# One attention kernel: maxima sent by SyncE, three score banks, one values bank, and new step offsets

## The reference, cut to what matters

```python
qh = q.reshape(b * h, d // h, m); kh = ...; vh = ...        # d = 128 channels, h = 8 heads of 16
qk = jnp.einsum('bdm,bdn->bmn', qh, kh) * scale             # 256 x 256 scores a head
sm = jax.nn.softmax(qk, axis=-1)
ret = jnp.einsum('bmn,bcn->bcm', sm, vh)
x = x + ret
```

## Time and profile before

| | us |
|---|---|
| median of 3 runs (451.76 to 454.36) | 451.77 |
| the profiled execution's own time | 453.62 |
| its span in the trace | 451.8 |
| start, up to the first transposed scores | 0 to 43.7 |
| the 128 steps and the end of the first block | 43.7 to 284 |
| choice of the tokens by digits | 284 to 326 |
| second attention and feed-forward | 326 to 451.8 |

### The profile page before, as it was taken

One profiled execution on the slowest core, in us unless ns is written; L12 is line 12 of the kernel. 1 busy time (PEld: TensorE's weight loads), 2 busy tenths in 40 slices (PEclk: granted clock), 3 DMA queues, 4 the chain that ended last, 5 costly groups with the idle time before them and its releaser, 6 DMA issues.

```text
span 451.8 us, 6847 instructions
## 1 busy us (share of the span) xinstructions
PE 293.6 (65%) x1888; PEld 185.2 (41%) x1888; DVE 298.2 (66%) x925; ACT 170.7 (38%) x413; POOL 113.1 (25%) x248
## 2 busy tenths in 40 slices
PE   0053764777667878767986764100157999999996
PEld 0011422343333443434442422000135888888884
DVE  6855565457666875768775453888747788878641
ACT  3201632334554465534354651000011455565622
POOL 1101662233322434222122221000013333332300
PEclk9999966668888695899685995555555799999999
DMA  3876584662925719245000047000000000000001
GB/s 97 194 186 113 137 166 83 155 107 93 159 49 146 135 51 180 54 114 111 0 2 1 3 127 245 1 1 0 0 0 1 1 23 2 23 23 23 23 25 46
DMA packets 24106, 32.80 MB, mean 73 GB/s; under 512 B 3915, under 2 KB 22158, under 8 KB 22542
## 3 DMA queue, kind: packets, MB, share of 16 engines
q1 hardware_dynamic: 23566, 32.34, 31.4%
q10 hardware_dynamic: 512, 0.13, 0.2%
HBM read 23.88 MB, written 8.39 MB: 71 GB/s over the span
## 4 chain that ended last, share of the span: by engine, by line
DVE 33%; PE 33%; issue 11%; DMA 8%; ACT 5%; ACTq 4%; POOL 4%; SPq 2%; DVEq 1%; POOLq 0%
PE pv_bank L1054 7%; DVE row_max L574 6%; DVE denom_inv L592 5%; PE scoret_bank L1040 4%; ACTq L886 4%; DMA q_stack<-q_parts_dram 4%; PE t_bank L1237 4%; PE score_bank L1027 4%; PE pv_bank L1155 3%; ACT probs L875 2%; DMA q_parts_dram<-q_parts 2%; PE score_bank L1218 2%; POOL rstd L390 2%; DVE junk L685 1%; DVE denom_own L596 1%
## 5 line engine op out<-in xcount | busy, mean ns | idle before, releaser
L574 DVE TENSOR_REDUCE row_max<-score_bank 128x2 f32<-128x512 f32 x112 | 73.5, 675 | 65.0 <-PE score_bank L1027 64.6
L875 ACT ACTIVATE probs<-scoret_bank 128x512 f32<-128x512 f32 x128 | 74.2, 600 | 77.0 <-issue 50.8
L1040 PE MATMUL scoret_bank<-q_stack,k_stack 98*128 98x256 bf16 x256 | 61.1, 332 | 53.4 <-ACT probs L875 44.5
L1027 PE MATMUL score_bank<-k_stack,q_stack 96*128 96x256 bf16 x240 | 57.7, 337 | 23.3 <-DMA q_stack<-q_parts_dram 16.1
L1040 PEld LDWEIGHTS scoret_bank<-q_stack,k_stack 98*128 98x128 bf16 x256 | 24.8, 114 | 75.7 <-ACT probs L875 57.6
L1054 PE MATMUL pv_bank<-probs,values_ones 128*32 128x256 f32 x512 | 48.6, 514 | 0.0
L1027 PEld LDWEIGHTS score_bank<-k_stack,q_stack 96*128 96x128 bf16 x240 | 21.4, 114 | 56.5 <-DVE row_max L574 21.5
L388 POOL TENSOR_SCALAR var_eps<-mv 128x1 f32<-128x1 f32 x48 | 9.1, 190 | 137.1 <-DVE mv L743 78.3
L1155 PE MATMUL pv_bank<-q_stack,k_stack 128*128 (+1 forms) x256 | 35.8, 283 | 0.4 <-ACT q_stack L1003 0.4
L978 ACT COPY xnt<-score_bank 128x256 f32<-128x256 f32 x16 | 6.0, 373 | 75.4 <-PE score_bank L1176 75.4
L1155 PEld LDWEIGHTS pv_bank<-q_stack,k_stack 128*128 128x128 f32 x256 | 33.7, 201 | 1.3 <-issue 0.9
(11 more groups left out here) (191 smaller groups left out, 542.2 us busy)
## 6 DMA issues: line engine op xcount, KB each, us to landing
q_stack<-q_parts_dram SPq DMA_DIRECT2D x48, 128.0 KB, 7.0
k_parts_dram<-k_parts SPq DMA_DIRECT2D x24, 128.0 KB
q_parts_dram<-q_parts SPq DMA_DIRECT2D x24, 128.0 KB
k_stack<-k_parts_dram SPq DMA_DIRECT2D x8, 384.0 KB, 4.9
ctx_stage<-in_ctx_dram SPq DMA_DIRECT2D x8, 256.0 KB, 3.3
x_stage<-in_x_dram SPq DMA_DIRECT2D x8, 256.0 KB, 4.2
k_stack<-k_parts_dram SPq DMA_DIRECT2D x8, 256.0 KB, 5.5
xs<-in_x_dram SPq DMA_DIRECT2D x8, 256.0 KB, 7.8
```

Source lines behind the costliest of these rows:

```text
L574: dve.tensor_reduce(row_max[:, i, :, h], score_bank[bank_of][:, :].rearrange("p (m n) -> p m n", m=2), AX.X, ALU.max).then_inc(s["max_done ...
L875: act.activation(probs[:, j % PROBS, :], scoret_bank[j % 2][:, :], ACT.Exp).then_inc(s["exp_done"], 1)
L1027: ins = pe.matmul(to[:, m * D:(m + 1) * D], q_stack[0:QROWS, slot, h, b_in, m * P:(m + 1) * P], k_stack[0:QROWS, slot, h, b_in, :], start= ...
L1040: ins = pe.matmul(scoret_bank[j % 2][:, k * D:(k + 1) * D], k_stack[0:SROWS, slot, h, b_in, k * P:(k + 1) * P], q_stack[0:SROWS, slot, h, ...
```

## The change

1. `send_neg_max` is issued by SP instead of ACT, with its place in SP's order two steps after `NEG_LOW`. SP's order is now one loop over the steps.
2. `score_bank` has three banks instead of two; a `scores` waits for the maximum three heads back. `pv_bank` is one bank instead of two, and the first `values` of a batch waits for `even_taken` of the batch before.
3. `take_even` copies the whole values bank to `pv_copy` in one instruction; a new `low_rows` on POOL masks it in two; `gather_parts` adds from `pv_copy`. The tensor `gathered` is gone, `low_part` takes its place.
4. Nearly all step offsets differ.

```diff
-MAX_T = {1: 1, 2: 9, 3: 15, **{b: NH * b - 13 for b in range(4, NB)}}
-STAGE = {3: 9, 4: 21, **{w: STEPS * (w - 3) for w in range(5, NU)}}
-SCALE_Q = {2: 1, 3: 11, 4: 24, **{w: STAGE[w] + 6 for w in range(5, NU)}}
-HIGH_Q = {2: 3, 3: 13, 4: 25, **{w: STAGE[w] + 7 for w in range(5, NU)}}
-MID_Q = {2: 5, 3: 15, 4: 27, **{w: STAGE[w] + 9 for w in range(5, NU)}}
+MAX_T = {1: 0, 2: 9, 3: 16, 4: 21, **{b: NH * b - 14 for b in range(5, NB)}}
+NEG_HIGH = {b: MAX_T[b] + 3 for b in MAX_T} | {1: 1}
+NEG_LOW = {b: MAX_T[b] + 2 for b in MAX_T} | {1: 1, 2: 10}
+STAGE = {3: 10, 4: 22, 5: 35, 6: 50, 7: 66}
+SCALE_Q = {2: 0, 3: 12, 4: 25, 5: 40, 6: 55, 7: 71}
+HIGH_Q = {2: 4, **{w: SCALE_Q[w] + 4 for w in STAGE}}
+MID_Q = {w: HIGH_Q[w] + 3 for w in HIGH_Q}
...
# SP
+            for t in range(LAST):
+                for b in due(NEG_LOW, t - 2):
+                    send_neg_max(b // 2, b % 2)
+                for w in due(MID_K, t):
+                    write_k_parts(w)
+                for w in due(MID_Q, t):
+                    write_q_parts(w)
+                    if w + 1 < NU:
+                        load_stage(w + 1)
+                for w in due(MID_Q, t - 2):
+                    load_stacks(w, w >= SLOTS)
+                if t % STEPS == STEPS - 4 and t // STEPS + 1 < NU:
+                    wait_apart(sp, s["x_loaded"], 16 * (t // STEPS + 1))
+                    load_x(t // STEPS + 1)
...
# POOL
+            def low_rows(b, i):
+                wait_apart(pool, s["even_taken"], b + 1)
+                pool.tensor_scalar(low_part[:, i, 0, :], pv_copy[:, i, 1, :], low[:, 0:1], None, ALU.mult)
+                pool.tensor_scalar(low_part[:, i, 1, :], pv_copy[:, i, 0, :], low[:, 0:1], None,
+                                   ALU.mult).then_inc(s["low_ready"], 1)
...
-                    if t == NH * b + 17:
+                    if t == NH * b + 18:
                         root_rows(b, b % 2)
...
+                    if t == NH * b + 9:
+                        low_rows(b, b % 2)
...
# DVE
             def gather_parts(b, i):
-                dve.wait_ge(s["even_taken"], b + 1)
-                if not (isinstance(b, int) and b < 2):
-                    dve.wait_ge(s["x1_done"], b - 1)
-                dve.scalar_tensor_tensor(gathered[:, i].rearrange("p k n -> p (k n)"), pv_bank[i][:, :], high[:, 0:1],
+                dve.wait_ge(s["low_ready"], b + 1)
+                dve.scalar_tensor_tensor(low_part[:, i].rearrange("p k n -> p (k n)"),
+                                         pv_copy[:, i].rearrange("p k n -> p (k n)"), high[:, 0:1],
...
# ACT
-                act.mul(low_part[:, i, 0, :], pv_bank[i][:, D:2 * D], low[:, 0:1])
-                act.mul(low_part[:, i, 1, :], pv_bank[i][:, 0:D], low[:, 0:1]).then_inc(s["even_taken"], 1)
+                act.copy(pv_copy[:, i].rearrange("p k n -> p (k n)"), pv_bank[:, :]).then_inc(s["even_taken"], 1)
...
-                for b in due(MAX_T, t - 3):
-                    send_neg_max(b // 2, b % 2)
...
# PE
-                    scores(score_bank[n % 2], n // STEPS, (n % STEPS) // NH, HEADS[n % NH], n - 1)
+                    scores(score_bank[n % 3], n // STEPS, (n % STEPS) // NH, HEADS[n % NH], n - 2)
...
-                    if not first:
-                        pe.wait_ge(s["div_step"], 4 * (b - 2) + 1)
+                    if b > 0:
+                        pe.wait_ge(s["even_taken"], b)
```

More of the change, by code:

```diff
@@ L213, in build_program @@
         out_rows = y
-        score_bank = [bank("score_bank0"), bank("score_bank1")]
+        score_bank = [bank("score_bank0"), bank("score_bank1"), bank("score_bank2")]
         scoret_bank = [bank("scoret_bank0"), bank("scoret_bank1")]
-        pv_bank = [bank("pv_bank0"), bank("pv_bank1")]
-        first_score_bank = score_bank + pv_bank
+        pv_bank = bank("pv_bank")
+        first_score_bank = score_bank + [pv_bank]
         t0_bank = bank("t0_bank")
@@ L268, in load_x, with send_neg_max @@
                 sp.dma_start(xs[:, bass.ds(2 * u, 2), :], x_rows[:, bass.ds(2 * u, 2), :]).then_inc(s["x_loaded"], 16)
+            def send_neg_max(u, i):
+                sp.wait_ge(s["neg_done"], 2 * u + i + 1)
+                for part in range(2):
+                    sp.dma_start(q_stack[QROWS + part:QROWS + part + 1, u % SLOTS, :, i, :],
+                                 neg_max[:, i, part, :]).then_inc(neg_loaded[i], 16)
             def write_k_parts(u):
@@ L323, in _ @@
             load_stacks(1, False)
-            sp.wait_ge(neg_loaded[0], 32)
+            send_neg_max(0, 0)
             load_x(0)
             load_small()
[L328 to L344, removed]
+            for t in range(LAST):
[12 more added lines that the diff above has]
+                    load_x(t // STEPS + 1)
             sp.wait_ge(s["scorest_ready"], STEPS * NU)
@@ L403, in add_x1 @@
                     wait_apart(pool, s["kept"], b - 1)
-                pool.tensor_tensor(x_new[:, i, :], gathered[:, i, 1, :], xs[:, b, :], ALU.add).then_inc(s["x1_done"], 1)
+                pool.tensor_tensor(x_new[:, i, :], low_part[:, i, 1, :], xs[:, b, :], ALU.add).then_inc(s["x1_done"], 1)
             def keep_rows(rows, b, i):
@@ L465, in _ @@
                 for b in range(NB):
-                    if t == NH * b + 14:
+                    if t == NH * b + 9:
+                        low_rows(b, b % 2)
+                for b in range(NB):
+                    if t == NH * b + 15:
                         add_x1(b, b // 2, b % 2, b < 2)
@@ L630, in stage_a @@
                             bring_over(b, i)
-                    for w in due(STAGE, t if t < STEPS * 2 else t - 1):
+                    for w in due(STAGE, t + 1 if t < STEPS * 2 else t):
                         stats_q(w)
@@ L634, in stage_a @@
                         scale_q(w)
-                    for b in due(MAX_T, t - 2):
+                    for b in due(NEG_LOW, t):
                         neg_low(b, b % 2)
@@ L881, in neg_high @@
                 act.mul(neg_max[:, i, 0, :], t0_bank[0:NH, 0:D], -1.0).then_inc(s["neg_hi"], 1)
-            def send_neg_max(u, i):
-                act.wait_ge(s["neg_done"], 2 * u + i + 1)
-                for part in range(2):
-                    act.dma_start(q_stack[QROWS + part:QROWS + part + 1, u % SLOTS, :, i, :],
-                                  neg_max[:, i, part, :]).then_inc(neg_loaded[i], 16)
             def take_vt(u):
@@ L939, in _ @@
             neg_high(0, 0, 0)
-            send_neg_max(0, 0)
             high_k(2)
-            for t in range(LAST + 3 * NH + 2):
+            for t in range(LAST + 3 * NH + 4):
                 if t < LAST:
@@ L947, in _ @@
                     i = b % 2
-                    if t == NH * b + 24:
+                    if t == NH * b + 27:
                         take_yw(b)
@@ L951, in _ @@
                         take_even(b, i, b < 2)
-                    if t == NH * b + 21:
+                    if t == NH * b + 24:
                         take_xnt(b, i, b < 2)
-                for b in due(MAX_T, t - 1):
+                for b in due(NEG_HIGH, t):
                     neg_high(b, b // 2, b % 2)
-                for b in due(MAX_T, t - 3):
-                    send_neg_max(b // 2, b % 2)
                 for w in due(STAGE, t):
@@ L1119, in _ @@
                 for b in range(NB):
-                    if t == NH * b + 20:
+                    if t == NH * b + 21:
                         if b > 0:
```

34 lines of the change are left out of this document (17 added, 17 removed).

## The result

The changed kernel took 459.15 us (median of 4 runs, 456.76 to 463.01), the kernel before 451.76 (4 runs beside it): a ratio of 1.0155, 95% interval 1.0103 to 1.0207. The forecast was 442 us, faster. The time lies just above the upper end of the range (427 to 459), where rival 3 was. The profiled execution took 458.6 us, with a span of 456.8 (before 453.62 and 451.8).

What follows compares the result with a forecast made beforehand. It took ACT's order, waiting to send the maxima and so holding PE, as the bound. Terms -3.9 (to unit 7), -5.3 and -2.5 (after), +2.1 (end) sum to -9.6 us: 442 us; range 427 to 459, the forecast's own 437 to 447.

Steps and rivals of the forecast that it cites:

- rival 3: Stacks come later still before a unit's first scores: chain 20.7 instead of 17.6 us, 457.5 us in all; chance 0.19.
- each head + 17.6: Predicted times of units 3 to 7 while stacks are awaited: 28.6, 28.8, 27.9, 27.0, 27.0 us; -3.9 us at unit 7.
- PE's head: Time from a unit's start to the last q part's cast: 9.4 us at the low clock, 11.0 for unit 3.
- the chain to the stacks: From that cast to landed stacks: cast, low part on POOL, write and landing 4.43, load 11.2; sum 17.6 us.
- the tail: Very end: values copied, masked by POOL, root and scaling ahead of the last gather_parts; 272.1 instead of 270.00, +2.1 us.
- The send: Maxima sent by SP: ACT loses a wait of about 3.9 us and 1.26 us of issue in each batch.
- The copy and GpSimd's mask: ACT gains 0.35 us a batch; POOL's masks, 0.95 us each, make DVE wait 0.9 us a batch for the root.
- After unit 7: No stack awaited: 16 steps take 22.4 instead of 27.7 us, -5.3; the last batches -2.5, the very end +2.1.
- Rival 2: GpSimd takes back ACT's gain: DVE waits 1.9 us a batch for the root and meets POOL more; 450 us, chance 0.25.

## Why the prediction was wrong

- **The step that failed: "each head + 17.6", with nothing in it for the masks.** I let PE's head and the chain to the stacks alone set the five units, and took the masks' wait as hidden in the wait for the stacks. In the sum the masks stand only in the unit after unit 7 (1.8 us) and in the tail. From the first scores of unit 2 to those of unit 7 that step gives 139.3 us (72.0 to 211.3). The changed kernel took 154.3 (71.22 to 225.49), and the same kernel with the masks on ACT 138.0. So the step holds without the masks on POOL, and the time too: 442.37 us, ratio 0.9837, where I had forecast 442, ratio 0.978, for the kernel with them. That is in part luck: in that run the chain took 18.4 to 18.8 us, and unit 3 took 31.2 us where I had 28.6.
- **The chain and the heads.** Where PE did wait for the stacks, in units 3, 4 and 7, the time from the cast to the scores was 20.5, 19.3 and 20.8 us instead of 17.6. In unit 7, 2.4 us of it are the write behind the send, and the head was 6.7 us instead of 9.4, so that the good number (27.51 us, 27.0 predicted) is two errors that cancel. In units 5 and 6, from 135.2 to 198.0 us, PE never waited for a stack, and still they took 32.1 and 30.7 us where I had 27.9 and 27.0 (26.9 and 27.6 with the masks on ACT). There ACT waited for the next unit's inputs, loaded right behind the write of the q parts, three or four steps before ACT needs them instead of four to seven. That wait, 26.4 us in five, stands nowhere in the prediction: I followed the moved cast to the stacks and not to the load that is tied to the same step. How much time it costs by itself stays open, since the old offsets keep 25.9 us of it and are 9 us faster.
- **The send: right, and too small.** "ACT loses a wait of about 3.9 us" and its two issues: gone as said, and this part alone gives 3.3%. What I missed is its new queue. I wrote that SP had room and counted only the write that stands behind a send. The send itself stands behind the stacks: 32.1 us of waits for `neg_max` in the kernel with only the send moved (8.9 before), and 15 us of time. The gain to be had from the send was 5.7 to 6.7%, not 3.3.
- **The copy and GpSimd's mask: the price right, the wait half of the truth.** A mask takes 0.93 to 0.94 us (0.95 taken). The wait I put at 0.9 us a batch, 14 in all. With the old offsets the masks raise it by 24.3 us (6.2 to 30.5), 1.5 us a batch, and with the new ones by 12.8 (18.3 to 31.1). The 2.8 to 3.2 us of DVE's own work that I counted as cover were there in some batches and not in others: at 213.33 us the scaling waits 0.53 us, at the end 2.16. The runs with and without masks show that this term is 13 to 18 us of time. The Trainium skill (GPSIMD Engine Reference, "Engine selection") would have one-input work roughly at line rate and so no wait at all; the measurement decides against it here. POOL takes 0.94 us for 128x256 by a column, where its own copy of that size takes 0.40 and DVE's scaling 0.41.
- **After unit 7: right.** To DVE's last `gather_parts` I had -5.3 - 2.5 + 2.1 = -5.7 us, and it became -5.0. The split was off: -8.5 and +3.5, in part because DVE's work moved over the cut; the clock in the first stretch was also better (0.88 instead of 0.75), and in the last batches DVE waits 2.16 us for the root, where no other work covers it. So the miss lies ahead of unit 7: -3.9 us predicted, +10.3 measured.
- **The rivals.** The time is rival 3's (457.5), and its mechanism, a chain of 20.7 us, held for units 3, 4 and 7 (20.5, 19.3 and 20.8), not for 5 and 6. Rival 2's mechanism carries the largest single term, at a larger price than rival 2 gave it. I treated them as alternatives. They were all present at once. One path of runs leads from the kernel before to the changed one, by the ratios: -0.033 for the send, -0.012 for the banks, the copy and the new `MAX_T` with the masks on ACT (not clear of noise), +0.039 for the masks on POOL, +0.021 for the offsets, together +0.0155 (such a path always closes). On another path the terms differ: the masks are +0.032 when they come last.

The rule on shared ports (the Trainium skill, SBUF — State Buffer, "Who interferes with whom") is seen three times in its two-input form, each time beside a `q_rest` that POOL had begun first. The longest, in the timeline of the changed kernel:

```profile
141.55 1.16 POOL L382 TENSOR_TENSOR q_rest<-qn,q_parts 128x512 f32<-128x512 f32 x1 [0.62 <-ACT q_parts L916]
141.73 1.53 DVE L597 SCALAR_TENSOR_TENSOR low_part<-pv_copy,high,low_part 128x512 f32<-128x512 f32 x1
...
267.21 0.75 DVE L597 SCALAR_TENSOR_TENSOR low_part<-pv_copy,high,low_part 128x512 f32<-128x512 f32 x1
```

Beside POOL the same instruction took 0.78 us longer; at 173.53 and 204.18 us it took 1.04 us. In the kernel before, with one input in PSUM, it took 0.74 us at 63.88 us beside a POOL instruction of 1.15 us. Over all 16 it averages 0.83 us against 0.74 before: 1.4 us in the whole kernel. The rule agrees with the trace and explains nothing of the loss.

**Open.** The three score banks, the single values bank and the new `MAX_T` were not run one by one, and the changed offsets with casts made sooner still had 31.1 us of waits for `neg_max`; the stacks behind the send was not tried on them. Whether a send comes late because it shares SP's queue with the stacks or because of the traffic beside it was not separated: ACT's sends go through a queue of their own (q10, 512 packets), SP's through the q1 of the stacks. In the run where ACT sends two steps later, one send was issued at 81.35 us beside the load of the stacks, and PE, which waited for it, went on at 88.54, 7.2 us later. So a queue of its own did not spare that send the delay.

## What to carry to other kernels

Moving an issue to an idle engine moves it behind that engine's transfers: list what is ahead of it and behind it on the new queue before counting the gain, and try the old engine with a later place first (one number gave 5.7% here). When a step is moved in a table, follow every transfer tied to it, the prefetch for the next unit too. An engine that is 25% busy is not free: work put ahead of a small result that the busiest engine waits for can cost much of its duration each time, here 30 us of POOL's work (1.9 us x 16) for 13 to 18 us of time. A wait that you take as hidden behind another one belongs into the sum with a reason and a row, above all where it comes in every unit.

## What I had not expected of the hardware

Two DMAs of 4 KB issued on SP right behind 1.5 MB of stacks and a load of 0.25 MB released PE 8.6 us after their issue; the DMA share was 0.91 between. GpSimd needs 0.94 us to multiply 128x256 by a column and 0.40 us to copy it.
